# A first layer norm transposed by VectorE squares and a DRAM buffer in place of TensorE, and three moves of single tiles, in a Macaron block (two feed-forward halves around attention) on one core

## The reference

```python
def reference(x, w_qkv, w_out, b_out, w1, b1, w2, b2):
    ffn  = lambda x: gelu(x @ w1 + b1) @ w2 + b2            # 256 -> 1024 -> 256, exact gelu
    def attn(x):                                            # 16 heads of 64
        q, k, v = split(x @ w_qkv)                          # q scaled by 1/8
        sim = q @ k.T - slope[h] * abs(i - j)               # ALiBi, causal mask
        return softmax(sim) @ v @ w_out + b_out
    x = x + 0.5 * ffn(layernorm(x))
    x = x + attn(layernorm(x))
    return x + 0.5 * ffn(layernorm(x))
```

## Time and profile before

| | |
|---|---|
| median of 3 runs | 2169.64 us (2169.27 to 2171.63) |
| profiled execution: its own time | 2169.53 us |
| profiled execution: span of its records | 2167.7 us |
| TensorE matmul busy | 2115.9 us, 98% of the span |
| VectorE / ScalarE / GpSimd busy | 1525.4 / 1272.0 / 1143.1 us |
| DMA | 209.70 MB, mean 97 GB/s |

### The profile page before, as it was taken

One profiled execution on the slowest core, in us unless ns is written; L12 is line 12 of the kernel. 1 busy time (PEld: TensorE's weight loads), 2 busy tenths in 40 slices (PEclk: granted clock), 3 DMA queues, 4 the chain that ended last, 5 costly groups with the idle time before them and its releaser, 6 DMA issues.

```text
span 2167.7 us, 42138 instructions
## 1 busy us (share of the span) xinstructions
PE 2115.9 (98%) x14480; PEld 1715.6 (79%) x14480; DVE 1525.4 (70%) x4121; ACT 1272.0 (59%) x3156; POOL 1143.1 (53%) x1988
## 2 busy tenths in 40 slices
PE   7999999999999999999999999999999999999998
PEld 6687787877878788787886878878787787877867
DVE  6776767767676676767767677676766777667674
ACT  5756656466565665756557465674646646565572
POOL 2754636546474563745547365473654637445361
PEclk9999999999999999999999999999999999999999
DMA  3432515234152342524425143251533415234142
GB/s 132 132 84 81 144 32 144 78 94 122 45 142 69 107 109 54 145 56 117 108 62 139 45 136 90 69 149 28 145 83 94 128 40 146 69 103 113 45 132 59
DMA packets 130294, 209.70 MB, mean 97 GB/s; under 512 B 42192, under 2 KB 70960, under 8 KB 130080
## 3 DMA queue, kind: packets, MB, share of 16 engines
q1 hardware_dynamic: 97888, 143.86, 23.6%
q0 software_dynamic: 25952, 58.38, 10.7%
q10 hardware_dynamic: 6240, 4.76, 0.8%
HBM read 14.95 MB, written 8.39 MB: 11 GB/s over the span
## 4 chain that ended last, share of the span: by engine, by line
PE 57%; DVE 19%; ACT 8%; issue 6%; POOL 4%; ACTq 3%; SPq 1%; DMA 1%; POOLq 0%; DVEq 0%
PE ps L361 56%; DVE P L937 5%; DVE gl L828 4%; ACT P L705 3%; ACTq L301 3%; DVE gh L896 2%; DVE xs L860 2%; POOL P L1126 2%; POOL PT L290 2%; DVE x L876 1%; DVE st L836 1%; SPq L290 1%; POOL rstd L1112 1%; ACT qk L651 1%; DVE xs L866 1%
## 5 line engine op out<-in xcount | busy, mean ns | idle before, releaser
L705 ACT ACTIVATE P<-P,mx 128x512 f32<-128x512 f32 (+3 forms) x1024 | 563.4, 553 | 281.6 <-DVE mx L929 281.4
L1126 POOL TENSOR_SCALAR P<-P,rs 128x512 f32<-128x512 f32 (+3 forms) x1024 | 539.2, 544 | 227.3 <-DVE rs L920 224.0
L290 POOL DMA_DIRECT2D PT<-P x646 | 324.1, 507 | 384.0 <-DVE P L937 361.1
L937 DVE STREAM_TRANSPOSE P<-P 128x1792 f32<-128x1792 f32 (+1 forms) x256 | 372.5, 1484 | 24.7 <-POOL P L1126 24.7
L361 PE MATMUL ps<-qk 64*128 64x512 f32 (+3 forms) x2048 | 321.3, 443 | 2.4 <-ACT qk L651 0.7
L361 PE MATMUL ps<-PT,v 128*64 128x256 f32 (+1 forms) x3072 | 306.7, 349 | 10.3 <-DMA PT<-P 8.7
L361 PE MATMUL ps<-w2h,gh 128*128 128x256 f32 x1024 | 291.9, 285 | 1.6 <-DVE gl L828 1.6
L361 PEld LDWEIGHTS ps<-PT,v 128*64 128x64 f32 x3072 | 204.3, 137 | 108.0 <-issue 17.1
L361 PE MATMUL ps<-w2l,gh 128*128 128x256 f32 x1024 | 289.7, 283 | 0.0
L361 PE MATMUL ps<-w2h,gl 128*128 128x256 f32 x1024 | 289.5, 283 | 0.0
L929 DVE CUSTOM_DVE_ANT_0 P<-ps,dist 128x512 f32<-128x512 f32 x256 | 166.1, 686 | 167.3 <-PE ps L361 166.8
(11 more groups left out here) (91 smaller groups left out, 4357.8 us busy)
## 6 DMA issues: line engine op xcount, KB each, us to landing
PT<-P SPq DMA_DIRECT2D x1392, 80.0 KB, 2.6
PT<-P POOLq DMA_DIRECT2D x646, 80.0 KB, 2.7
x<-in_L_attn_x SPq DMA_DIRECT2D x16, 512.0 KB, 4.4
out_y<-x SPq DMA_DIRECT2D x15, 512.0 KB, 2.9
xt<-xs SPq DMA_DIRECT2D x195, 32.0 KB, 2.0
xt<-xs POOLq DMA_DIRECT2D x165, 32.0 KB, 1.9
xt<-xs ACTq DMA_DIRECT2D x120, 32.0 KB, 2.2
raw<-in_L_ffn_w SPq DMA_DIRECT2D x2, 512.0 KB, 5.7
```

Of the source, the lines that this page charges most:

```text
L290: e.dma_start(PT[c % 2][32 * m:32 * m + 32, g, :], P[c % 3][32 * g:32 * g + 32, m, :]).then_inc(landed.sem, 16)
L705: e.activation(p, p, ACT.Exp, bias=mx[:, r, i:i + 1], scale=-1.0, accum_out=sm[:, r, i:i + 1]).then_inc(s_ex.sem, 1)
L937: e.transpose(p, p).then_inc(s_tr.sem, 1)
L1126: e.tensor_scalar(p, p, rs[:, 2 * (c % 2) + h, i:i + 1], 1.0, ALU.mult, ALU.mult).then_inc(s_nz.sem, 1)
```

## The change

Four parts. (1) Layer norm 1 of batches 1 to 15 no longer goes over TensorE: `stats` and `power` move from step 4 to step 3, `normal` (into `xs[1]`) from step 5 to step 4, followed by a new `turned_x`; SP writes the 512 KB of `xs[1]` to a DRAM buffer `rows_out` after `spread` of step 3 and reads them back with four DMAs of 128 KB after `spread` of step 4; `ln_hi` waits for those. The two `ln_transpose` are gone. (2) The first down tile takes a bank of (6, 7) and not 5. (3) ScalarE copies step 6's first V tile ahead of `exps(b, 6, 2)`, not behind it. (4) In the last batch `out_part(0)` and `(1)` come ahead of `values(5)`, `(2)` and `(3)` behind it, with their splits moved accordingly.

```diff
-    xs = place("xs", [128, 4, NK, NT, 32], F32, PT_AT)
+    xs = {L: place(f"xs{L}", [128, 4, NK, NT, 32], F32, a) for L, a in ((1, XN), (2, PT_AT), (3, PT_AT))}
+    rows_out = nc.dram_tensor("rows_out", [128, 4, NK * NT * 32], F32, kind="Internal").ap()
-    by_dma = [(L, b) for L, b in lns if (L == 2 and b > 0) or (L == 3 and b < NB - 1)]
+    by_dma = [(L, b) for L, b in lns if (L < 3 and b > 0) or (L == 3 and b < NB - 1)]
+    def rows_through_dram_out(e, b):
+        if b > 1:
+            e.wait_ge(s_ri.sem, s_ri.at((1, b - 1)))
+        e.wait_ge(s_xr.sem, s_xr.at((1, b, 0)))
+        e.dma_start(rows_out[:, :, :],
+                    xs[1][:, :, :, :, :].rearrange("p m k t s -> p m (k t s)")).then_inc(s_ro.sem, 16)
+    def rows_through_dram_in(e, b):
+        e.wait_ge(s_gs.sem, s_gs.at((2, b - 2, NM - 1)) if b > 1 else s_gs.at((1, 0, NM - 1)))
+        e.wait_ge(s_ro.sem, s_ro.at((1, b)))
+        for m in range(4):
+            e.dma_start(xt[32 * m:32 * m + 32, :, :, :, :].rearrange("s g k t r -> s g (k t r)"),
+                        rows_out[:, m, :].rearrange("(g s) n -> s g n", g=4)).then_inc(s_ri.sem, 16)
@@ SP, after spread of step c
+                    if c == 3 and b + 1 < NB:
+                        rows_through_dram_out(e, b + 1)
+                    if c == 4 and b + 1 < NB:
+                        rows_through_dram_in(e, b + 1)
@@ TensorE, begin
-                    among[0] = (5,)
+                    among[0] = (6, 7)
                     dn(2, b - 1, 0)
@@ TensorE, attention
-                    if more and c == NC - 2:
-                        ln_transpose(1, b + 1, 0)
-                        among[0] = (5,)
-                        ln_transpose(1, b + 1, 1)
-                        among[0] = (6, 7)
-                    values(b, c - 2)
+                    if more or c < NC - 1:
+                        values(b, c - 2)
@@ TensorE, last batch
-                    among[0] = range(4)
-                    for c in range(4):
-                        out_part(c, range(NT))
-                    among[0] = range(4, 8)
+                    among[0] = (0, 1, 6, 7)
+                    turn[0] = 7
+                    out_part(0, range(NT))
+                    out_part(1, range(NT))
+                    among[0] = range(2, 6)
+                    values(b, NC - 3)
+                    out_part(2, range(NT))
+                    out_part(3, range(NT))
-            among[0] = (6, 7)
+            among[0] = (2, 3)
             ln_transpose(3, NB - 1, 0)
@@ ScalarE, ln_hi and attention
+                if (L, b) in by_dma and L == 1:
+                    e.wait_ge(s_ri.sem, s_ri.at((L, b)))
+                    if not more and c == NC - 1:
+                        out_part_hi(0)
+                        out_part_hi(1)
-                    exps(b, c, 2)
+                    if c != NC - 2:
+                        exps(b, c, 2)
                     for tile in steps_v(b, c)[:1]:
                         proj_copy(b, tile)
+                    if c == NC - 2:
+                        exps(b, c, 2)
@@ VectorE, attention
+                    if not more and c == NC - 1:
+                        out_part_lo(0)
+                        out_part_lo(1)
-                    if more and c == 4:
+                    if more and c == 3:
                         e.wait_ge(s_x.sem, s_x.at(b + 1))
                         for t in range(NT):
                             stats(1, b + 1, t)
                         variance(1, b + 1)
-                    if more and c == 5:
+                    if more and c == 4:
                         for t in range(NT):
                             normal(1, b + 1, t)
+                        turned_x(1, b + 1, range(NT))
@@ GpSimd, attention
-                        if c == 4:
+                        if c == 3:
                             power(1, b + 1)
```

More of the change, by code:

```diff
@@ L198, in build @@
     stats_units = [k for L, b in lns
-                   for k in ([(L, b, 0), (L, b, 1)] if (L, b) in by_halves or (L, b) in by_dma else [(L, b, None)])]
+                   for k in ([(L, b, 0), (L, b, 1)] if (L, b) in by_halves or (L > 1 and (L, b) in by_dma) else [(L, b, None)])]
     def share(L, b, u):
@@ L203, in share @@
             return range(NT)
-        n = NT - 1 if (L, b) in by_dma else NT // 2
+        n = NT - 1 if (L, b) not in by_halves else NT // 2
         return range(n, NT) if u else range(n)
@@ L275, in build @@
     s_xs = {L: Signal(f"xn_spread{L}", [k for k in by_dma if k[0] == L], 16 * len(X_SP[L])) for L in (2, 3)}
+    s_ro = Signal("rows_out_done", [k for k in by_dma if k[0] == 1], 16)
+    s_ri = Signal("rows_in_done", [k for k in by_dma if k[0] == 1], 16 * 4)
     s_xa = {L: Signal(f"xn_spread_act{L}", [k for k in by_dma if k[0] == L], 16 * len(X_ACT[L])) for L in (2, 3)}
@@ L301, in spread_x @@
             e.dma_start(xt[32 * m:32 * m + 32, g, :, :, :],
[L302 removed]
+                        xs[L][32 * g:32 * g + 32, m, :, :, :]).then_inc(landed.sem, 16)
+    def rows_through_dram_out(e, b):
[10 more added lines that the diff above has]
+                        rows_out[:, m, :].rearrange("(g s) n -> s g n", g=4)).then_inc(s_ri.sem, 16)
     block = nc.Block()
@@ L653, in ln_hi @@
             def ln_hi(L, b, u):
-                if (L, b) in by_dma:
+                if (L, b) in by_dma and L == 1:
+                    e.wait_ge(s_ri.sem, s_ri.at((L, b)))
+                elif (L, b) in by_dma:
                     e.wait_ge(s_xs[L].sem, s_xs[L].at((L, b)))
@@ L759, in attention @@
                 else:
-                    for c in range(2):
+                    for c in (2, 3):
                         out_part_hi(c)
                     spread(e, b, NC - 2, LAST_ACT, s_la[NC - 2])
-                    for c in range(2, 5):
-                        out_part_hi(c)
+                    out_part_hi(4)
                     out_copy(b, NC - 3)
@@ L854, in normal @@
                         e.wait_ge(s_ll.sem, s_ll.at((*by_dma[n - 1], 1)))
-                    dst, src = xs[:, :, :, t, :], src.rearrange("p (k m s) -> p m k s", k=NK, m=4)
+                    dst, src = xs[L][:, :, :, t, :], src.rearrange("p (k m s) -> p m k s", k=NK, m=4)
                 else:
@@ L864, in turned_x @@
                 e.wait_ge(s_xn.sem, s_xn.at((L, b, ts.stop - 1)))
-                p = xs[:, :, :, :, :].rearrange("p m k t s -> p (m k) (t s)")[:, :, 32 * ts.start:32 * ts.stop]
+                p = xs[L][:, :, :, :, :].rearrange("p m k t s -> p (m k) (t s)")[:, :, 32 * ts.start:32 * ts.stop]
                 e.transpose(p, p).then_inc(s_xr.sem, 1)
@@ L1010, in attention @@
                 else:
-                    out_part_lo(0)
-                    out_part_lo(1)
+                    out_part_lo(2)
+                    out_part_lo(3)
                 turned(b, NC - 1, 1)
@@ L1017, in attention @@
                 if not more:
-                    for c in range(2, NC):
+                    for c in range(4, NC):
                         out_part_lo(c)
```

## The result

The changed kernel takes 2186.47 us, the median of 4 runs (2181.20 to 2193.62), beside 2170.64 for the kernel before (4 runs, 2169.27 to 2175.18). The ratio is 1.0071, with a 95% interval of 1.0039 to 1.0104: slower by 15.8 us between the medians. The profiled execution is the fastest of the four, 2181.20, with a span of 2179.4, 11.7 more than before.

What follows compares the result with a forecast made beforehand. The prediction took ScalarE, VectorE and SP to set the start of values(6), so TensorE's saved transposes count nothing. Sum: 2169.5 - 12.0 + 7.4 - 3.5 + 4.8 + 7.7 - 1.0 = 2172.9 us, range 2155 to 2187.

Steps and rivals of the forecast that it cites:

- Slower: The outcome of a time above the no-change band, which ended at 2174.0 us; given a chance of 0.38.
- no change: The outcome of a time from 2165.3 to 2174.0 us; given a chance of 0.31.
- a sign that it had named for being wrong: The clock falling in the middle batches, one of three listed observations that would make the forecast wrong.
- What bounds values(6): In front of values(6): ScalarE, VectorE and SP set its start, so removing TensorE's transposes gains 0.0.
- Down tile's bank: At scores(b, 1): no more wait for bank 5, 0.8 us in each of fifteen batches, -12.0; bounds 0 and 12.4.
- Copy of V: At exps(6, 2): the earlier copy ends step 6's exps later in eight batches, +7.4, and earlier in seven, -3.5.
- ln_lo, +4.8: In ln_lo: two subtractions per batch, both inputs in SBUF beside GpSimd, each take 0.16 us longer; bounds 0 and 12.
- Steps 3 and 4: On VectorE: late x and added work delay GpSimd's late issue by 1.1 us in seven batches, +7.7; bounds 0 and 14.
- DRAM path: Ahead of ln_hi: rows land 8 to 10 us after step 6's scores, wanted at 10.8: 0; bounds 0 and +9.
- Last batch: At values(5): two output shares fill the 2.90 us wait, -1.0; bounds 0 and -2.9.
- The clock, rival 4: At the new 2.0 us wait: the clock falls, giving 2195 in all fifteen batches, 2184 in half; chance 0.12.
- The pause, rival 3: At GpSimd's step 4: its pause goes away with the power ahead of it, or moves, giving 2161; chance 0.20.

Runs made afterwards that it cites:

- e1: The kernel before with only the first down tile's bank changed, from 5 to one of (6, 7): 2202.25 us, ratio 1.0145.
- e7: The changed kernel with load_x of the next batch issued ahead of the spread of step 1 on SP, not behind it: 2178.50 us, ratio 1.0036.
- e5: The kernel before with the first down tile in bank 7 alone in place of 5, so later tiles keep their banks: 2158.38 us, ratio 0.9939.
- e8: The changed kernel with eight identity transposes on TensorE ahead of values(4) in fifteen batches, overwritten by values(4): 2197.14 us, ratio 1.0113.
- e2: The changed kernel with step 6's first V copy behind exps(6, 2) again: 2190.71 us, ratio 1.0085.
- e6: The changed kernel without the five DRAM DMAs per batch, ln_hi and ln_lo reading xs[1], so computing something else: 2199.67 us, ratio 1.0128.
- e12: The kernel before with the first down tile in bank 7 and the last batch's new order: 2156.66 us, ratio 0.9940.
- e9: The changed kernel with GpSimd's addition of b2 to x at the end of its step 7, not step 6: 2197.03 us, ratio 1.0124.
- e11: The changed kernel with x loaded ahead of step 1's spread, b2 added in GpSimd's step 7, and SP issuing all spread DMAs for three steps: 2192.23 us, ratio 1.0101.
- e3: The changed kernel with the last batch's order as before: 2197.31 us, ratio 1.0124.

## Why the prediction was right or wrong

The forecast was 2172.9 and the median is 2186.5, inside the range and just under its upper end. Slower had the highest chance of the three. The forecast itself was 13.6 too low, and that the time is in the range is in part luck: 2172.9 stood in what the prediction called no change, the -12.0 came out only beside part 1 (e1), and a sign that it had named for being wrong was seen, a fall of the clock in the middle batches. Beside the profiled execution, the sum gave +3.4 and the traces show +11.7. Means over batches 1 to 14, odd and even, in us after scores(6) or after the step before:

| | before | changed | e7 | e5 |
|---|---|---|---|---|
| end of exps(6) | 9.92 / 11.89 | 10.87 / 12.21 | 10.86 / 11.84 | 9.91 / 11.90 |
| from there to turned(6, 1) | 1.72 / 1.72 | 2.15 / 2.63 | 1.97 / 2.63 | 1.72 / 1.72 |
| start of turned(6, 1) to end of turned(6, 0) | 4.13 / 4.13 | 4.13 / 4.13 | 4.12 / 4.12 | 4.13 / 4.13 |
| values(6) after scores(6) | 24.89 / 26.87 | 26.13 / 28.00 | 26.05 / 27.67 | 24.87 / 26.82 |

- **What bounds values(6)**: right. The transposes were worth 0.0: with them gone TensorE waits 1.7 to 2.3 at values(6) or at the first up tile, and eight put back (e8) change nothing but the wait.
- **Down tile's bank, -12.0**: right in size (-11.2 over 14 batches; e5 in full). The working was incomplete: its bounds held no word on the rotation of banks 6 and 7. By e1 the same edit costs 31 us where the transposes are kept. It came out here only because part 1 takes a tile from the rotation.
- **Copy of V, +7.4 and -3.5**: right for the odd batches, +0.95 (0.93 forecast). In the even ones the row above is +0.32, where this term and that of steps 3 and 4 together were +0.6. With values(4) now in the bank of that V tile, e2 without the move gained nothing.
- **ln_lo, +4.8**: the step that failed. Measured +0.43 in odd and +0.91 in even batches, 8 x 0.43 + 7 x 0.91 = 9.8, and this is with no subtraction kept out for long (0.08 of the 0.43 is the one wait for late rows, below). I took the stretch of 0.16 from one row, of a subtraction in another place beside other operations of GpSimd. Taking turns, each waits for a whole operation of the other, which was my upper bound, 12. Beyond it stands what no row of before showed: 3.0 to 4.6 for one subtraction in 9 of 90 batches of six traces. The rule of the Trainium skill, SBUF — State Buffer, Who interferes with whom, by which the prediction had this term at 12 and the time at 2180, was nearer than the row. Its wording, that whoever issues first keeps the other out for the whole instruction, fits the turns; the long waits pass over five GpSimd instructions (e8) and it does not state them.
- **Steps 3 and 4, +7.7**: the size is near, the place only in part. The even batches' +0.32, with the 0.50 that the copy gives back there (e2), is 0.82, so 5.7 in seven; x late costs 1.8 more in steps 2 to 6, in odd batches too (batch 11 has 1.2). Of the 5.7, e7 takes away 7 x 0.37 = 2.6; the rest stays with x in time. e7 is 8.0 below the changed kernel's median, its trace 4.0 below the other. The rest of e7's gain shows in no trace of the changed kernel. e7's trace has no long subtraction and three falls of the clock fewer; that either is the rest is argued only.
- **DRAM path, 0**: near. The rows land 8.6 to 11.4 after scores(6) (8 to 10 forecast, wanted at 10.8): a single wait of 0.5 in the profile, up to 1.7 in others. Five of the nine long subtractions came right behind late rows. e6 shows that the rest of the excess stays without the path.
- **Last batch, -1.0**: measured +1.2 in the profile, nothing in e12. The wait moved from values(5) to values(6), as the sum's own warning on the last two values said.
- **The clock, rival 4**: came in part, and the sum had it at nothing. It fell in six places of batches 1 to 14, after waits of 1.9 to 2.5, and held after others as long (2.3 in batches 10 and 12). In batch 0 it fell behind 2.23, and in e5 in the same place behind 1.95, where the kernel before held behind 1.97: the length of the one wait doesn't tell. values(6) of batch 1 took 4.05, and that batch and batch 13 lost 1.6 and 1.5 behind it; some 3 us of the 11.7 by these two, the other falls not priced. The Trainium skill, TensorE: Matmul & The Clock Gate, HAM oscillation, describes a loop that waits for a DMA in each pass, longer than here, and has the clock fall in every one; here it fell in seven of fifteen batches.
- **The pause, rival 3**: wrong. The power, 1.03 before, is gone from its place, and GpSimd waits 4.11 there and not 3.15, so that the issue follows its last `normalise` by about as much as before. Against the scores of step 6 it stands 0.6 to 1.2 later than before, as VectorE is late there.

The median lies 5.3 above the profiled execution. One to two long subtractions of 3.4 each would make it, and three or four the slowest run. No trace of those runs exists, so this is argued and not shown; e6's trace, 9.6 longer without a long subtraction, and its slow runs say that there is more in it.

## What to carry to other kernels

When a tile is taken out of a rotation of banks, or put into one, write down for every later tile whose bank it gets: here that was worth more (31 us in e1) than everything else in the change. Work that leaves an engine gives only what its next wait leaves; move a step from PSUM to SBUF on VectorE beside GpSimd only after looking for the longest such operation in the trace, and price it by a whole operation of the other engine. When a step is moved earlier, move its load too, if the queue has room ahead of the transfer that it stands behind (8 us between the medians in e7, 4 between the traces).

## What the runs showed that I had not expected

- A VectorE subtraction with both inputs in SBUF takes 0.68 alone, 0.84 to 1.25 when it takes turns with GpSimd's operations, 1.70 to 2.06 when it meets a GpSimd addition of 2.4, and 3.0 to 4.6 when it gets no turn until GpSimd's row has ended (2.3 where the row is shorter, in e9 and once in e11). Which it is differs between batches of the same program.
- GpSimd's pause of 3 us at a DMA issue comes first at its 129th DMA, and from the second on it keeps its place in the program when 15 earlier DMAs go to another queue.
- The same program up to the last batch reached scores(15, 0) at 2034.9 and 2047.2 in two traces (the changed kernel and e3).
